# First attention of a chain of layers: first two head groups scored in fp32 on 32-row tiles, reads by group, causal mask by GpSimd selects, value products woven into the scores

## The chip, the cores and the metric

The program runs on one core of one Trainium2 chip. The time is the device time of one execution in microseconds; the median of several runs is compared. Engines are called PE (TensorE; PEld is its weight load), DVE (VectorE), ACT (ScalarE), POOL (GpSimd) and SP (SyncE, which issues most DMAs).

## What is computed

The reference is a chain of eight residual layers on one tensor x of 4 x 512 tokens and 128 channels. Only the first layer is touched by the change, a causal softmax attention with 16 heads of 8 channels (block-wise in the reference, which gives the same result):

```python
xn = layernorm(x)
q, k, v = (heads(xn @ W.T) for W in (Wq, Wk, Wv))      # 4 x 16 x 512 x 8
s = 8 ** -0.5 * q @ k^T, masked where the key is later than the query
x = x + (exp(s - max s) @ v / sum) @ Wo.T
```

Everything is fp32. The layers behind it (two mixtures of experts, a feature attention, a gated recurrence, a retention and two quantized feed-forward layers) stay as they are.

## The kernel before, in words

Each engine has a program of its own, written out by hand; the order of the calls in `attn_a_tensor`, `attn_a_vector`, `attn_a_scalar`, `attn_a_gpsimd` and `attn_a_sync` is the order of the work, and semaphores tie them. b is the batch block (4 of 512 tokens), a group n is four heads of one block (n // 4 the block, n % 4 the four heads), so there are 16 groups.

**Start.** For each b: layer norm on DVE (`norm_front` statistics, `norm_root` on POOL, `norm_back` with L117), transposes on PE (L127), copy by ACT (L135), projections of q and k (L168, `factors`) with channels as rows, copied by ACT (L448). The scores use bf16 with three terms: q and k are split into three bf16 parts (block 0 by DVE, L347 to L353, in line with its norms; blocks 1 to 3 by POOL, L518 to L524), written to a DRAM scratch (L558, L560) and read back (L546, L551), so that all 72 products of parts and channels of one head lie in 72 rows of `a_QS` and `a_KS`. Block 0 is read by group, blocks 1 to 3 whole: 1152 KB for q and three times 384 KB for k.

**One group.** `maxima` (L194, then L197) computes scores with queries as rows into PSUM bank 6 or 7 in turn, eleven jobs for a group, and adds the causal mask by a matmul of the identity with `neg_ts`; DVE reduces each job (L359) to its maximum, and its job frees the bank. `maxima_split` (L368 to L374) splits the maxima in three bf16 parts, `rows` transposes them (L208), `row_copy` (L381) copies them, and SP's `rows` brings them by three small DMAs (L583) into rows 72 to 74 of `a_QS`. Then `exps` and `tail` (L214) compute the scores with keys as rows, less the maximum, in banks 0 to 3 and 4, `late` (L218) adds the mask with `neg_st`, and ACT takes the exponential (L465, L470) into `a_PT`, six buffers. `values` (L252) multiplies with v and a column of ones, sixteen products on four 32-column tiles in one lump, into bank 5; ACT evicts (L478), `turned` transposes (L264), DVE normalizes (L388 to L392).

**The loop.** PE first computes the maxima of groups 0 and 1. Iteration n then scores group n, with the jobs of maxima n + 2, `rows(n + 1)`, `values(n - 1)` and `turned(n - 1)` between. DVE's list has the same order. Once for each block there are also the projection of v (`plain`), `back` (L273) and `output` (L282), the residual (L143) and the next layer's norm. SP's list in `attn_a_sync` is: rows(n + 1), then the write of block n + 2 (n = 0, 1), then the read of block 2 or 3 (n = 3, 7, after the last scores of the block two before). At its start SP loads x in four DMAs and then `pack_zero`, 2653.5 KB of constants for later layers, first read at `expert_bias` at the end of iteration 14.

Of the kernel before, what the change touches and what calls it, by code (L numbers as in the profile page):

```python
# [21 lines left out]
          "r_km": "a_f", "r_v": "a_exped", "r_ot": "a_ol", "r_raw": "a_ot", "f_rowt": "a_rowt"}  # L22
# [131 lines left out]

def side(M):

    M.sides[0] += 1
    return 6 + M.sides[0] % 2


def attn_a_tensor(pe, S, M):
    def factors(b):
        for name, w, bk in (("q", M.a_wq, 2 + 2 * (b % 2)), ("k", M.a_wk, 3 + 2 * (b % 2))):
            made = S["a_proj"]
            take(pe, M, bk)
# [46 lines left out]
    def scores(b, h, si, out, first=True):  # L212
        i = b % 2
        pe.matmul(out, M.a_KS[0:75, i, h, 128 * si:128 * si + 128], M.a_QS[0:75, i, h, 128 * si:512], start=first, stop=False, skip_group_check=True)  # L214

    def late(out):

        return pe.matmul(out, M.identb[:, :], M.neg_st[:, :].unsqueeze(1).to_broadcast([128, out.shape[1], 128]), start=False, stop=True,  # L218
                         skip_group_check=True)

    def exps(n, hh):
# [2531 lines left out]
```

## Time and profile before

| | |
|---|---|
| median of 3 runs | 1253.16 us (1251.23 to 1256.07) |
| profiled execution, its own time | 1249.02 us |
| its span | 1247.2 us |
| mean granted PE clock | 0.867 |
| busy PE / DVE / ACT / POOL | 1007.8 / 835.9 / 387.6 / 294.5 us |
| first attention in it | 0 to about 268.4 us |
| PE's granted clock by fortieths of the span, first ten | 8 6 8 9 9 8 9 9 8 9 tenths |

The granted clock is a share of 2.4 GHz; 0.50 is 1.2 GHz. A stretch with a value between has parts at either level. A busy engine is not an engine at its peak: PE's busy time counts overlapping matmuls once.

### The profile page before, as it was taken

To read this page: it belongs to the slowest core of one execution; us is meant where nothing else is said; L and a number is where in the kernel's file an instruction comes from. 1 tells how busy PE (TensorE), PEld (TensorE's weight loads), DVE (VectorE), ACT (ScalarE), POOL (GpSimd) and SP (SyncE) were. 2 spreads that over 40 slices of the span, in tenths; PEclk is the share of its full clock that TensorE was granted. 3 is DMA by queue.
4 is the path that set the end of the run, shared out by engine and by line. 5 is a ranking of instruction groups with operands and counts; after the bars stand their busy time and mean duration, and the time that the engine had idled before them with its cause. 6 is when DMAs were issued, how large, how long until landed. Compare 5 with 4: busy or idle time off the path is not lost.

```text
span 1247.2 us, 16823 instructions
## 1 busy us (share of the span) xinstructions
PE 1007.8 (81%) x6275; PEld 619.5 (50%) x6275; DVE 835.9 (67%) x2001; ACT 387.6 (31%) x634; POOL 294.5 (24%) x249
## 2 busy tenths in 40 slices
PE   3798988979989897679897862999999566897465
PEld 2254555543434565543333331776768345676344
DVE  5666758756565467767666566648555896688895
ACT  1154445533333243423232254112211222231121
POOL 3600000003222433303222213121110344233232
PEclk8689889989999787779888896899999887787786
DMA  8633030020000000000000000000000000000000
GB/s 239 161 103 78 2 78 2 3 89 1 1 1 0 1 2 1 2 1 0 1 1 0 1 0 3 1 1 1 1 1 2 0 1 1 2 2 2 1 9 25
DMA packets 9948, 25.40 MB, mean 20 GB/s; under 512 B 979, under 2 KB 7315, under 8 KB 9171
## 3 DMA queue, kind: packets, MB, share of 16 engines
q1 hardware_dynamic: 9568, 23.49, 6.6%
q10 hardware_dynamic: 294, 0.79, 0.3%
q8 instruction: 52, 0.85, 0.3%
q14 instruction: 34, 0.28, 0.1%
HBM read 16.73 MB, written 7.34 MB: 19 GB/s over the span
## 4 chain that ended last, share of the span: by engine, by line
PE 54%; DVE 31%; issue 6%; ACT 4%; POOL 3%; DMA 2%; DVEq 0%; SPq 0%; ACTq 0%; POOLq 0%
PE ps L686 5%; DVE a_MN L359 4%; PE ps L673 4%; PE ps L678 4%; PE ps L252 3%; PE ps L194 2%; DVE XN L117 2%; PE ps L1507 2%; PE ps L1568 2%; PE ps L1522 2%; PE ps L1565 2%; PE ps L2098 2%; PE ps L214 2%; PE ps L1940 2%; POOL rs L96 1%
## 5 line engine op out<-in xcount | busy, mean ns | idle before, releaser
L359 DVE TENSOR_REDUCE a_MN<-ps 128x1 f32<-128x384 f32 (+3 forms) x176 | 107.4, 639 | 59.6 <-PE ps L197 57.5
L96 POOL TENSOR_TENSOR rs<-t,mhalf 128x4 f32<-128x4 f32 x37 | 37.4, 1011 | 382.8 <-DVE t L90 382.5
L930 POOL TENSOR_TENSOR f_Y<-f_Y,f_TT 128x512 f32<-128x512 f32 x56 | 70.8, 1265 | 179.4 <-DVE f_TT L820 179.4
L465 ACT ACTIVATE a_PT<-ps 128x1024 f32<-128x1024 f32 x64 | 65.1, 1024 | 69.9 <-PE ps L218 68.9
L895 ACT ACTIVATE f_HH<-ps,pack_zero 128x512 f32<-128x512 f32 x64 | 44.0, 687 | 132.9 <-PE ps L673 132.9
L143 DVE TENSOR_TENSOR X<-ps,X 128x512 f32<-128x512 f32 x32 | 22.0, 687 | 92.7 <-PE ps L1578 49.4
L194 PE MATMUL ps<-a_KS,a_QS 72*128 72x128 bf16 (+3 forms) x256 | 70.5, 337 | 14.1 <-DVE a_MN L359 10.9
L686 PE MATMUL ps<-f_HH,pack_zero 128*128 128x512 f32 x128 | 73.9, 660 | 5.7 <-DVE f_TT L820 5.7
L811 DVE TENSOR_TENSOR f_XS<-ps,XNT 128x512 f32<-128x512 f32 x64 | 43.9, 688 | 49.2 <-PE ps L666 49.2
L673 PE MATMUL ps<-f_XS,pack_zero 128*128 128x512 f32 x128 | 69.9, 630 | 1.3 <-DVE f_XS L811 1.3
L820 DVE SCALAR_TENSOR_TENSOR f_TT<-ps,pack_zero,f_X 128x512 f32<-128x512 f32 x64 | 47.9, 749 | 32.5 <-PE ps L686 32.5
L1921 PE MATMUL ps<-pack_one,XNT 128*128 128x352 f32 x128 | 50.0, 539 | 23.4 <-DVE q_HH L1970 23.2
L678 PE MATMUL ps<-f_XS,pack_zero 128*128 128x512 f32 x128 | 68.5, 618 | 0.0
L214 PE MATMUL ps<-a_QS,a_KS 75*128 75x128 bf16 (+3 forms) x256 | 58.2, 316 | 6.1 <-DMA a_QS<-a_MT 5.9
L1940 PE MATMUL ps<-pack_one,q_HT 128*128 128x128 f32 (+1 forms) x192 | 36.1, 334 | 20.9 <-ACT q_HT L2023 20.9
L899 ACT ACTIVATE f_X<-ps 128x512 f32<-128x512 f32 x64 | 38.2, 597 | 33.0 <-PE ps L679 32.9
L1921 PEld LDWEIGHTS ps<-pack_one,XNT 128*128 128x128 f32 x128 | 27.1, 225 | 41.3 <-DVE q_HH L1970 27.6
L197 PE MATMUL ps<-pack_half 128*128 128x128 bf16 (+2 forms) x176 | 47.3, 269 | 0.0
L194 PEld LDWEIGHTS ps<-a_KS,a_QS 72*128 72x128 bf16 x256 | 23.2, 105 | 43.6 <-DVE a_MN L359 27.7
L1940 PEld LDWEIGHTS ps<-pack_one,q_HT 128*128 128x128 f32 (+1 forms) x192 | 29.3, 228 | 30.4 <-ACT q_HT L2023 23.4
L127 PE MATMUL ps<-pack_first,XN 128*128 128x128 f32 x80 | 16.5, 343 | 33.8 <-DVE XN L117 33.8
L252 PE MATMUL ps<-a_PT,a_VA 128*32 128x128 f32 (+3 forms) x512 | 42.2, 464 | 1.3 <-ACT a_PT L470 1.3
(310 smaller groups left out, 2322.4 us busy)
## 6 DMA issues: line engine op xcount, KB each, us to landing
scratch<-a_parts SPq DMA_DIRECT2D x16, 384.0 KB, 4.3
a_QS<-scratch SPq DMA_DIRECT2D x3, 1152.0 KB
a_KS<-scratch SPq DMA_DIRECT2D x9, 384.0 KB
pack_one<-in_one SPq DMA_DIRECT2D x1, 2679.5 KB, 9.3
pack_zero<-in_zero SPq DMA_DIRECT2D x1, 2653.5 KB, 16.3
a_QS<-scratch SPq DMA_DIRECT2D x4, 288.0 KB
a_KS<-scratch SPq DMA_DIRECT2D x12, 96.0 KB
X<-in_x SPq DMA_DIRECT2D x4, 256.0 KB, 10.1
```

What stands on the lines that cost most here:

```text
L96: pool.tensor_tensor(M.rs[:, 4 * b:4 * b + 4], M.t1[:, 4 * b:4 * b + 4], M.mhalf[:, 0:4], ALU.pow).then_inc(root.sem, root.tick(n, b))
L194: pe.matmul(bank(M, bk, N, N * u), M.a_QS[0:72, i, h, 128 * ti:128 * ti + 128], M.a_KS[0:72, i, h, 0:N], start=(u == 0), stop=False, skip_ ...
L214: pe.matmul(out, M.a_KS[0:75, i, h, 128 * si:128 * si + 128], M.a_QS[0:75, i, h, 128 * si:512], start=first, stop=False, skip_group_check= ...
L252: m = pe.matmul(bank(M, 5, N, 128 * si, 32 * j, 32 * j + 32), M.a_VA[:, i, si, 4 * g + j, :], M.a_PT[:, (4 * n + j) % 6, A_AT[si]:A_AT[si] ...
L359: dve.tensor_reduce(M.a_MN[:, n % 2, ti, h0:h0 + k], bank(M, M.bank["a_max", n, jj], 128 * (ti + 1) * k).rearrange("p (a c) -> p a c", a=k ...
L465: act.activation(M.a_PT[:, c % 6, 0:1024], M.ps[:, a * 512:a * 512 + 1024], ACT.Exp).then_inc(made.sem, made.tick(n, hh))
L673: pe.matmul(bank(M, 2 + u % 2), M.f_w1[:, e, :], M.f_XS[:, x, :], start=True, stop=True).then_inc(made.sem, made.tick(n, u, 1))
L678: pe.matmul(bank(M, 4), M.f_w3[:, e, :], M.f_XS[:, x, :], start=True, stop=False)
L686: pe.matmul(bank(M, 5), M.f_w2[:, e, :], M.f_HH[:, u % 3, :], start=True, stop=True).then_inc(made.sem, made.tick(n, u))
L930: pool.tensor_tensor(M.f_Y[:, i, :], M.f_Y[:, i, :], M.f_TT[:, u % 3, :], ALU.add).then_inc(made.sem, made.tick(n, u))
L1921: pe.matmul(bank(M, 2 * k + s, 352), M.XNT[:, 128 * t:128 * t + 128], M.WG[:, s, :], start=True, stop=True).then_inc(made.sem, made.tick(n ...
L1940: m = pe.matmul(bank(M, bo, 128, 128 * (t % 4)), M.q_HT[0:rows, t % 2, a, :], M.WD[0:rows, a, :], start=(a == 0), stop=(a == 2))
```

## The change

Five things change together in the first attention:

1. Groups 0 and 1 (block 0, heads 0 to 7) are computed without the bf16 parts and without DRAM. `own` projects q and k so that head j of the group lies in rows 32j to 32j + 7 of a tile; ACT copies them with a scale that zeroes the other rows and, for k, a bias that makes row 32j + 8 a row of ones. `own_maxima` multiplies in fp32 on 32-row tiles of PE (group 0 four heads at a time in banks 4 to 7, group 1 two in banks 6 and 7). DVE writes the maxima into column 32j + 8 of `a_MX`, fp32 transposes turn them (`own_rows`), and `own_add` adds them as row 32j + 8 of q. `own_exps` and `own_tail` score in fp32 on the same tiles.
2. Block 0's groups 2 and 3 and all later blocks still go through DRAM, but POOL now splits block 0 too, and every read is of one group (`a_spread`); for groups 8 to 15 it stands behind rows(n + 1) of iteration n = group - 5. `pack_zero` is loaded in three parts behind the rows DMAs of groups 12 to 14.
3. The mask matmuls on the scores (`late`) are gone; POOL zeroes the masked part of the exponentials instead (`seen`: per group four selects of 128 x 256 and two of 128 x 512 elements).
4. `a_PT` has eight buffers for six; `values(n - 1)` is divided into its four key blocks, one behind each head's scores; `turned`, `evict` and `normalize` come one iteration later, and `back`, `output`, `residual`, the transposes of the next layer likewise one group later.
5. At the start DVE computes the statistics of all blocks first; the norm, transposes and projections of blocks 2 and 3 are placed between the groups.

The core of the diff ("..." where left out):

```diff
+    def own(g, name, bk):
+        made, w = S["a_proj"], M.a_oq if name == "q" else M.a_ok
+        M.bank["a_own", g, name] = bk
+        take(pe, M, bk)
+        pe.matmul(bank(M, bk), w[:, 8 * g:8 * g + 128], M.XNT[:, 0:512], start=True, stop=True).then_inc(made.sem, made.tick("own", g, name))
+        M.freed[bk] = (S["a_own"], (g, name))
...
+    def own_maxima(n, part, heads, banks):
+        maxed = S["a_maxed"]
+        for j, bk in zip(heads, banks):
+            M.bank["a_max", n, part, j] = bk
+            take(pe, M, bk)
+        pe.wait_ge(S["a_own"].sem, S["a_own"].at(n, "k"))
+        at = 0
+        for ti in A_FIRST[part]:
+            N = 128 * (ti + 1)
+            for j, bk in zip(heads, banks):
+                row = slice(32 * j, 32 * j + 8)
+                pe.matmul(bank(M, bk, N, at), M.a_Q4[row, n, 128 * ti:128 * ti + 128], M.a_K4[row, n, 0:N],
+                          start=(at == 0), stop=False, skip_group_check=True)
+            at += N
+        for j, bk in zip(heads, banks):
+            tiles = bank(M, bk).rearrange("p (a c) -> p a c", a=4)
+            ends = (tiles[:, 3:4, :], tiles[:, 0:4:3, :], tiles[:, 1:2, :])[part]
+            k = len(A_FIRST[part])
+            pe.matmul(ends, M.identb[:, :], M.neg_ts[:, :].unsqueeze(1).to_broadcast([128, k, 128]), start=False, stop=True,
+                      skip_group_check=True).then_inc(maxed.sem, maxed.tick(n, part, "own", j))
+            M.freed[bk] = (S["a_reduced"], (n, part, "own", j))
...
+    def own_scores(n, j, si, out):
+        row = slice(32 * j, 32 * j + 9)
+        return pe.matmul(out, M.a_K4[row, n, 128 * si:128 * si + 128], M.a_Q4[row, n, 128 * si:512], start=True, stop=True)
...
+    def own_exps(n, half):
+        scored = S["a_scored"]
+        for bk in range(4):
+            take(pe, M, bk)
+        pe.wait_ge(S["a_mt"].sem, S["a_mt"].at(n))
+        for u in range(2):
+            own_scores(n, 2 * half + u, 0, bank(M, 2 * u))
+        for u in range(2):
+            own_scores(n, 2 * half + u, 1, bank(M, 2 * u + 1, 384))
+        for u in range(2):
+            hh = 2 * half + u
+            own_scores(n, hh, 3, bank(M, 2 * u + 1, 128, 384)).then_inc(scored.sem, scored.tick(n, hh))
+            M.freed[2 * u] = M.freed[2 * u + 1] = (S["a_exped"], (n, hh))
...
+        if jj == 0:
+            pe.wait_ge(S[f"a_spread{n % 4}{i}"].sem, S[f"a_spread{n % 4}{i}"].at(b))
...
         scores(b, h, 0, bank(M, a))
-        late(bank(M, a, 128).unsqueeze(1))
         scores(b, h, 1, bank(M, a + 1, 384))
-        scores(b, h, 3, bank(M, a + 1, 128, 384), False)
-        late(bank(M, a + 1).rearrange("p (a c) -> p a c", a=4)[:, 0:4:3, :]).then_inc(scored.sem, scored.tick(n, hh))
...
+    def values(n, si):
+        b, g, i, valued, N = n // 4, n % 4, n // 4 % 2, S["a_valued"], 512 - 128 * si
+        if si == 0:
+            take(pe, M, 5)
+            if g == 0:
+                pe.wait_ge(S["a_va"].sem, S["a_va"].at(b))
+            pe.wait_ge(S["a_seen"].sem, S["a_seen"].at(n, "tail", 1))
+        for j in range(4):
+            m = pe.matmul(bank(M, 5, N, 128 * si, 32 * j, 32 * j + 32), M.a_VA[:, i, si, 4 * g + j, :],
+                          M.a_PT[:, (4 * n + j) % 8, A_AT[si]:A_AT[si] + N],
+                          start=(si == 0), stop=(si == 3), skip_group_check=True)
+        if si == 3:
+            m.then_inc(valued.sem, valued.tick(n))
+            M.freed[5] = (S["a_ol"], (n,))
...
+    own_maxima(0, 0, range(4), range(4, 8))
+    factor(0, "q", 3)
+    factor(0, "k", 0)
+    own_maxima(0, 1, range(4), range(4, 8))
+    own(1, "q", 1)
+    own(1, "k", 2)
+    own_maxima(0, 2, range(4), range(4, 8))
+    plain(0, 3)
+    turn_tensor(pe, S, M, 0, 1, 0, M.XN, (S["normed"], (0, 1)))
+    factor(1, "q", 1)
+    factor(1, "k", 2)
+    own_rows(0, 5)
+    own_exps(0, 0)
+    own_maxima(1, 0, (0, 1), (6, 7))
+    own_tail(0, 0, 0)
+    own_maxima(1, 0, (2, 3), (6, 7))
+    own_tail(0, 0, 1)
+    own_maxima(1, 1, (0, 1), (6, 7))
+    own_exps(0, 1)
+    own_maxima(1, 1, (2, 3), (6, 7))
+    own_tail(0, 1, 0)
+    own_maxima(1, 2, (0, 1), (6, 7))
+    own_tail(0, 1, 1)
+    own_maxima(1, 2, (2, 3), (6, 7))
+    own_rows(1, 5)
+    turn_tensor(pe, S, M, 0, 2, 0, M.XN, (S["normed"], (0, 2)))
+    factor(2, "q", 2)
+    factor(2, "k", 3)
     pe.wait_ge(S["in_ones"].sem, 16)
     for jj in range(11):
-        maxima(0, jj)
-    for jj in range(6):
-        maxima(1, jj)
-    rows(0)
+        maxima(2, jj)
+    own_exps(1, 0)
+    maxima(3, 0)
+    own_tail(1, 0, 0)
+    values(0, 0)
+    own_tail(1, 0, 1)
+    maxima(3, 1)
+    values(0, 1)
+    plain(1, side(M))
+    for jj in range(2, 6):
+        maxima(3, jj)
+    rows(2)
+    own_exps(1, 1)
+    values(0, 2)
+    own_tail(1, 1, 0)
+    values(0, 3)
+    own_tail(1, 1, 1)
     for jj in range(6, 11):
-        maxima(1, jj)
...
+        maxima(3, jj)
+    turn_tensor(pe, S, M, 0, 3, 0, M.XN, (S["normed"], (0, 3)))
+    factor(3, "q", 2)
+    factor(3, "k", 3)
+    for n in range(2, 16):
+        b, g, ahead = n // 4, n % 4, range(11) if n + 2 < 16 else range(0)
+        for hh in range(4):
+            for jj in ahead[3 * hh:3 * hh + 1]:
+                maxima(n + 2, jj)
+            exps(n, hh)
+            for jj in ahead[3 * hh + 1:3 * hh + 2]:
+                maxima(n + 2, jj)
+            if hh % 2:
+                tail(n, hh // 2)
+            if hh == 1 and n + 1 < 16:
+                rows(n + 1)
+            values(n - 1, hh)
+            for jj in ahead[3 * hh + 2:3 * hh + 3]:
+                maxima(n + 2, jj)
+            if hh == 0 and g == 1 and b + 1 < 4:
+                plain(b + 1, side(M))
+            if hh == 0 and g == 2 and b:
+                back(b - 1)
+            if hh == 1:
+                turned(n - 2)
+            if hh == 2 and g == 2 and b:
+                output(b - 1)
+            if hh == 3 and g == 3 and b:
+                turn_tensor(pe, S, M, 1, b - 1, side(M), M.XN, (S["normed"], (1, b - 1)))
+    turned(14)
+    for si in range(4):
+        values(15, si)
...
+    norm_back(dve, S, M, 0, 1, M.X, M.XN)
+    norm_back(dve, S, M, 0, 2, M.X, M.XN)
+    for part in range(3):
+        for j in range(4):
+            own_reduce(0, part, j)
+    own_add(0)
+    for part in range(3):
+        for j in range(4):
+            own_reduce(1, part, j)
+    own_add(1)
+    norm_back(dve, S, M, 0, 3, M.X, M.XN)
     for jj in range(11):
-        reduce(0, jj)
-    maxima_split(0)
+        reduce(2, jj)
+    maxima_split(2)
     for jj in range(6):
-        reduce(1, jj)
-    row_copy(0)
+        reduce(3, jj)
+    row_copy(2)
     for jj in range(6, 11):
-        reduce(1, jj)
-    maxima_split(1)
-    for n in range(16):
+        reduce(3, jj)
+    maxima_split(3)
+    for n in range(2, 16):
         b, g, more = n // 4, n % 4, n + 2 < 16
         if more:
-            for jj in range(6):
+            for jj in range(5):
                 reduce(n + 2, jj)
         if n + 1 < 16:
             row_copy(n + 1)
+        if more:
+            reduce(n + 2, 5)
+        if g == 3 and b:
+            norm_back(dve, S, M, 1, b - 1, M.X, M.XN)
+        normalize(n - 2)
...
+    def own(g):
+        made, proj = S["a_own"], S["a_proj"]
+        act.wait_ge(proj.sem, proj.at("own", g, "q"))
+        act.activation(M.a_Q4[:, g, :], bank(M, M.bank["a_own", g, "q"]), ACT.Identity, scale=M.a_o3[:, 0:1]).then_inc(made.sem, made.tick(g, "q"))
+        act.wait_ge(proj.sem, proj.at("own", g, "k"))
+        act.activation(M.a_K4[:, g, :], bank(M, M.bank["a_own", g, "k"]), ACT.Identity, bias=M.a_o3[:, 2:3],
+                       scale=M.a_o3[:, 1:2]).then_inc(made.sem, made.tick(g, "k"))
...
+    def seen(n, half):
+        made, c = S["a_seen"], 4 * n + 2 * half
+        for u in range(2):
+            P = M.a_PT[:, (c + u) % 8, 0:1024].rearrange("p (a t) -> p a t", a=2)[:, :, 0:128]
+            pool.wait_ge(S["a_exped"].sem, S["a_exped"].at(n, 2 * half + u))
+            pool.affine_select(P, P, [[0, 2], [1, 128]], ALU.is_ge, 0.0, base=0, channel_multiplier=-1).then_inc(made.sem, made.tick(n, 2 * half + u))
+        P = M.a_PT[:, c % 8:c % 8 + 2, 896:1152].rearrange("p h (a t) -> p h a t", a=2)
+        pool.wait_ge(S["a_exped"].sem, S["a_exped"].at(n, "tail", half))
+        pool.affine_select(P, P, [[0, 2], [0, 2], [1, 128]], ALU.is_ge, 0.0, base=0, channel_multiplier=-1).then_inc(made.sem, made.tick(n, "tail", half))
...
+    for b in range(2):
         split(b, "q")
         split(b, "k")
-    for b in range(4):
-        norm_root(pool, S, M, 1, b)
+    for n in range(2):
+        for half in range(2):
...
+    written(0)
+    read(2)
+    read(3)
     write(1)
-    read(1)
-    rows(0)
-    for n in range(15):
+    written(1)
+    for n in range(4, 8):
+        read(n)
+    for n in range(1, 15):
         rows(n + 1)
-        if n in (0, 1):
-            write(n + 2)
-        if n in (3, 7):
-            read(n // 4 + 2)
+        if n in (1, 2):
+            write(n + 1)
+        if n == 3:
+            written(2)
+        if n == 7:
+            written(3)
+        if 3 <= n < 11:
+            read(n + 5)
+        if n >= 11 and n < 14:
+            zeros(n - 11)
...
```

## Rows read from the trace of the kernel before

**Rows 1.** Busy time by stretches: us; PE, PEld, DVE, ACT, POOL; clock, DMA share, GB/s.

```profile
11.25:41.00 29.75, 16.70 (x38) 7.80 (x39) 17.17 (x59) 6.46 (x11) 13.62 (x16) 0.73 0.81 261
...
41.00:59.10 18.10, 14.70 (x64) 4.96 (x62) 15.38 (x28) 0.60 (x1) 10.59 (x12) 0.59 0.62 132
...
59.10:83.40 24.30, 22.94 (x160) 13.96 (x159) 15.87 (x35) 11.55 (x14) 0.00 (x0) 0.79 0.35 114
...
239.50:268.40 28.90, 24.70 (x213) 18.06 (x214) 14.74 (x67) 12.63 (x18) 2.01 (x2) 0.86 0.13 46
```

**Rows 2.** Timeline of the start: start us, us, operation, [idle before <-releaser].

```profile
22.94 1.11 PE L127 MATMUL ps<-pack_first,XN 128*128 128x128 f32 x4 [7.10 <-DVE XN L117]
...
37.26 3.75 PE L168 MATMUL ps<-XNT,pack_first 128*128 128x512 f32 x4 [0.78 <-ACT XNT L135]
...
39.96 0.15 PEld L194 LDWEIGHTS ps<-a_KS,a_QS 72*128 72x128 bf16 x1 [0.52 <-issue]
```

**Rows 3.** Timeline: first scores of iterations 2, 3, 14; values and reduce in 2.

```profile
83.34 0.38 PE L214 MATMUL ps<-a_QS,a_KS 75*128 75x512 bf16 x1
...
87.67 2.32 PE L252 MATMUL ps<-a_PT,a_VA 128*32 128x512 f32 x29
...
90.35 0.56 DVE L359 TENSOR_REDUCE a_MN<-ps 128x1 f32<-128x384 f32 x1 [2.00 <-PE ps L197]
...
94.57 0.38 PE L214 MATMUL ps<-a_QS,a_KS 75*128 75x512 bf16 x1
...
240.55 0.38 PE L214 MATMUL ps<-a_QS,a_KS 75*128 75x512 bf16 x1
```

**Rows 4.** Groups by line, 83 to 239.7 us: | busy, mean ns | idle before.

```profile
L359 DVE TENSOR_REDUCE a_MN<-ps 128x1 f32<-128x512 f32 (+3 forms) x133 | 81.3, 639 | 43.6 <-PE ps L197 42.1
...
L218 PE MATMUL ps<-pack_half 128*128 128x256 bf16 (+1 forms) x120 | 31.5, 262 | 0.0
...
L381 DVE COPY a_MT<-ps 12x512 bf16<-12x512 bf16 x12 | 4.9, 412 | 0.5 <-PE ps L208 0.4
...
L392 DVE TENSOR_TENSOR a_ON<-ps,a_RS 128x128 f32<-128x128 f32 x12 | 3.5, 291 | 0.4
...
L390 DVE RECIPROCAL a_RS<-a_RS 128x16 f32<-128x16 f32 x12 | 3.0, 253 | 0.4
...
L117 DVE TENSOR_SCALAR XN<-X,mv,rs 128x128 f32<-128x128 f32 x8 | 2.2, 343 | 0.1
...
L370 DVE TENSOR_TENSOR a_MR<-a_MN,a_M 128x16 f32<-128x16 f32 x12 | 2.1, 175 | 0.4
```

**Rows 5.** The chain that ended last: start us, us, what.

```profile
112.09 8.85 DMA a_QS<-a_MT
...
168.81 9.17 DMA a_QS<-a_MT
```

**Rows 6.** Timeline of SP's queue.

```profile
104.83 0.33 SPq L546 DMA_DIRECT2D a_QS<-scratch  x1
```

**Rows 7.** Busy time by stretches of 2 us, at the first stall.

```profile
118.00:120.00 2.00, 0.27 (x2) 0.00 (x0) 1.49 (x6) 0.00 (x0) 0.00 (x0) 1.00 0.41 88
```

**Rows 8.** Timeline, PE's weight loads, another stage.

```profile
428.86 1.78 PEld L978 LDWEIGHTS ps<-pack_zero,p_QT 32*128 32x128 f32 x16 [1.50 <-issue]
...
430.87 1.78 PEld L989 LDWEIGHTS ps<-pack_zero,XNT 128*128 128x128 f32 x8 [0.23 <-issue]
```

**Rows 9.** Groups by line and shape, POOL, whole span.

```profile
L1261 POOL TENSOR_SCALAR p_PK<-p_XW 128x512 f32<-128x512 f32 x16 | 23.8, 1490 | 45.5 <-ACT p_XW L1180 45.0
...
L2362 POOL COPY r_VA<-pack_zero 128x128 f32<-128x128 f32 x16 | 4.9, 348 | 6.2 <-ACT pack_zero L2319 6.2
```

**Rows 10.** Timeline, DVE beside POOL's split.

```profile
31.59 3.66 DVE L117 TENSOR_SCALAR XN<-X,mv,rs 128x128 f32<-128x128 f32 x4
...
41.91 4.07 DVE L359 TENSOR_REDUCE a_MN<-ps 128x4 f32<-128x512 f32 x7 [6.66 <-PE ps L197]
...
49.46 1.01 DVE L372 CAST a_M<-a_MR 128x16 bf16<-128x16 f32 x1
```

More of the change, by code:

```diff
@@ L180, in maxima, with own_tail @@
+    def own_tail(n, half, u):
+        scored, landed = S["a_scored"], S["a_landed"]
+        if u == 0:
+            take(pe, M, 4)
+            own_scores(n, 2 * half, 2, bank(M, 4, 256)).then_inc(landed.sem, landed.tick(n, half))
+        else:
+            pe.wait_ge(landed.sem, landed.n)
+            own_scores(n, 2 * half + 1, 2, bank(M, 4, 256, 256)).then_inc(scored.sem, scored.tick(n, "tail", half))
+            M.freed[4] = (S["a_exped"], (n, "tail", half))
     def maxima(n, jj):
@@ L210, in rows, with scores @@
         M.freed[bk] = (S["a_mt"], (n,))
-    def scores(b, h, si, out, first=True):
+    def scores(b, h, si, out):
         i = b % 2
[L214 to L219, printed above, removed]
+        return pe.matmul(out, M.a_KS[0:75, i, h, 128 * si:128 * si + 128], M.a_QS[0:75, i, h, 128 * si:512], start=True, stop=True)
     def exps(n, hh):
@@ L497, in attn_a_scalar @@
             tail(n, half)
-            if half == 0:
-                if n:
-                    evict(n - 1)
-                if g == 0 and b + 1 < 4:
-                    plain(b + 1)
-                if g == 1 and b:
-                    back(b - 1)
-                if g == 3 and b:
-                    turn_scalar(act, S, M, 1, b - 1)
+            if n == 1 and half == 0:
+                plain(1)
+        turn_scalar(act, S, M, 0, n + 2)
+        factors(n + 2)
+    for n in range(2, 16):
+        b, g = n // 4, n % 4
+        evict(n - 2)
+        exps(n, 0)
+        if g == 1 and b + 1 < 4:
+            plain(b + 1)
+        if g == 2 and b:
+            back(b - 1)
+        exps(n, 1)
+        tail(n, 0)
+        exps(n, 2)
+        exps(n, 3)
+        tail(n, 1)
+        if g == 3 and b:
+            turn_scalar(act, S, M, 1, b - 1)
+    evict(14)
     evict(15)
@@ L533, in attn_a_gpsimd @@
         norm_root(pool, S, M, 0, b)
-    for b in range(1, 4):
+    for b in range(2):
         split(b, "q")
         split(b, "k")
-    for b in range(4):
-        norm_root(pool, S, M, 1, b)
+    for n in range(2):
+        for half in range(2):
+            seen(n, half)
+        split(n + 2, "q")
+        split(n + 2, "k")
+    for n in range(2, 16):
+        b, g = n // 4, n % 4
+        for half in range(2):
+            seen(n, half)
+        if g == 2 and b:
+            norm_root(pool, S, M, 1, b - 1)
+    norm_root(pool, S, M, 1, 3)
 def spread_rows(sp, b, name, scr, dst, done, event, heads=slice(0, 16)):
```

243 lines of the change are left out of this document (104 added, 139 removed).

## The prediction, made before the change was run

> **What bounds the kernel now.** I read the busy time by stretches first, because the change touches only the first attention, 0 to 268.4 us of the 1247.2 us span. The reader should see four stretches in [rows 1]: the start to the first maxima (11.25 to 41.0), the maxima of groups 0 and 1 ahead of the loop (to 59.1), iterations 0 and 1 (to 83.4), and the tail (239.5 to 268.4, 28.9 us). TensorE (PE) was granted 0.73, 0.59 and 0.79 in the first three: much of the start ran at 1.2 GHz.
>
> Then the timeline of the start [rows 2]. PE sat idle 7.10 us before block 1's transposes, because VectorE (DVE) splits q and k of block 0 before it normalizes block 1. But the first maxima's weights load at 39.96, straight behind the last projections (37.26 plus 3.75), with no wait for a DMA. So the bounce through DRAM is not what the start waits for; the order of work on PE and DVE is.
>
> Then one iteration [rows 3]. The first scores of iterations 2 and 3 start 11.23 us apart, those of iteration 14 at 240.55. So iterations 2 to 13 took 157.2 us: 12 x 11.23 = 134.8, and 22.4 more. In each iteration the values matmuls are one lump of 2.3 us, and DVE idles 2.00 us behind it. The groups by line [rows 4] give DVE's own work in one iteration: eleven reduces 6.7 us (81.3 x 11 / 133), row copy 0.41, normalize 0.25 + 0.29 and a small one as the split's (0.175), split 4 x 0.175: 8.5, and 8.9 with the gaps of 0.03 to 0.05 between dependent ones.
>
> Last the stalls: the chain holds two row DMAs of 8.85 and 9.17 us [rows 5]. SP issued the read of block 2 at 104.83 [rows 6], 2.3 MB, and DMA was still at 0.41 busy in 118 to 120 [rows 7]; the 12 KB of rows(5) queued behind it. No scores of iteration 5 could start before they landed.
>
> **The change, part by part.**
> *Start.* The DVE split goes to POOL, which nobody needs before group 2. The first own projections start at 11.25 as the others do now and take 3.75, as in [rows 2]; with ScalarE's (ACT) copy of 0.6 they are there at 15.6. A maxima job of four 32-row tiles is a cost the trace lacks. The nearest rows [rows 8]: 16 weight loads of 32-row fp32 pairs took 1.78 us, 8 loads of full fp32 tiles the same 1.78 us, so a pair costs what one full matmul costs. I take tiles of different rows as parallel: 1.0 us for 512 columns at 2.4 GHz and 2.0 at 1.2, for a pair or for four; the other end is one after the other, 0.49 us more for each further tile and pass pair. Part 0 is thus done at about 18; DVE by then has normalized blocks 1 and 2. Three parts go back and forth between PE (2.3, 1.9, 1.3 at mixed clock) and DVE (6.7 in all), with projections between: the reduces end at 29. Values projection 1, transposes 1.1, copy 0.6, projections of block 1 3.2, row transposes 1 and the add 0.7: the scores of group 0 start at 36.5, where they started at 59.1.
> *Groups 0 and 1.* What was gained is then spent. Scoring one group costs 6.2 us of PE in fp32 (per half 2.1 for the pairs plus 1.0 for two single tails) where bf16 took some 3. Group 1's maxima come in pairs, and each pair must be reduced (two heads, 1.4 us, plus 0.25 of latency) before the next enters banks 6 and 7: with the scores between them 17 to 18 us for this section. Then, each in PE's line: transposes and projections of block 2 (3.4), the maxima of group 2 (8), the scores of group 1 woven with values 0 and the maxima of group 3 (16), and block 3 (3.2). Sum: 36.5 + 17.7 + 3.4 + 8 + 16 + 3.2 = 85, and 2 for stretches at 1.2 GHz: iteration 2 starts at 87, 4 later than now. Bounds: 77 if little of the alternation shows, 95 if it is all at 1.2 GHz.
> *Steady loop.* Ten mask matmuls go: 31.5 us over 12 iterations by busy time, some 0.85 us of streaming in each. They are PE's, and DVE has the longer list, so alone they would give little. The weave gives more: the 2.3 us lump becomes pieces of 0.9, 0.65, 0.45 and 0.2. Walking one iteration, PE may do about 0.4 us of other work between two maxima jobs without starving DVE (a reduce of 0.6 to 0.69 less a job of 0.2 to 0.3). Over it are the first piece (hidden under the split), the second with rows and tail (0.25 us of DVE idle), and turned (0.1). So 8.9 + 0.5 to 0.7: 9.5. Two costs come on top. Values of n-1 wait for POOL's last select: exp ends, 0.1 later the select, then PE. An affine select is in no row; the nearest one-input POOL rows are a copy of 128 elements at 348 ns and a TENSOR_SCALAR of 512 at 1490 ns [rows 9]. By these ends 256 elements cost 0.35 to 0.75 us or, by an operation slower than both, more. I take 0.5 for 256 and 0.9 for 512, nearer to the copy since nothing is computed but a choice: the values start some 0.5 late, 0.4 of it felt. And POOL, now 4 x 0.5 + 2 x 0.9 = 3.8 us busy in each iteration, can hold DVE (next part): 0.2. That makes 10.1.
> *Extras in iterations 2 to 13.* Residual, norm front and back for two blocks (some 4 each, of which the four normalize instructions 1.4 [rows 4]), plain projections and the wait of normalize 0 for POOL's split of block 3: 12. Total 12 x 10.1 + 12 = 133 against 157.2.
> *Reads.* They move to quarters (576 KB, at 14.5 us per 2.3 MB about 3.6 us) behind rows(n+1) in SP's queue; each is done about when the next rows are issued, 10 us later. SP's wait before group 8's read (end of iteration 3) is over before row copy 5. I cost them at nothing, covered by some 1 us of slack; at the other end 0.5 us in each of 8 iterations. The 2.65 MB of constants move behind rows 12 to 14, in three parts of some 5 us; needed at the end of iteration 14: nothing.
> *Tail.* Iterations 14 and 15 have no maxima and stay as now: from 240.55 [rows 3] to 268.4, the end of the last stretch in [rows 1], 27.9. The last select stands before values 15: +0.5, so 28.4.
>
> Sum: start 87 + 133 + 28.4 = 248.4 against 268.4: **20 us less**. The profiled execution took 1249.0 (span 1247.2); the median of three is 1253.2. It stands 4 above, so I forecast 1253.2 - 20 = **1233** and give all times on the median's scale.
>
> **The rule weighed.** In [rows 10] DVE's four normalize instructions took 3.66 us and one 16-element cast 1.01 us while POOL split q and k; the same take 4 x 0.343 and 0.175 elsewhere [rows 4]. Seven reduces out of PSUM beside the same POOL work took 4.07, 0.58 each, no more than their mean of 0.64. My sum has 0.2 us an iteration for it, since POOL is busy for 3.8 of 10; without it the sum gives 1231, and with every second split instruction held 1251 (a rival below). The Trainium skill (SBUF — State Buffer, section "Who interferes with whom") says that a DVE copy, cast or tensor_scalar and a GpSimd instruction lock each other out for a whole instruction, and tensor_reduce never; by that rule, the trace agrees, and the selects are a cost to DVE and not only to POOL.
>
> **Rivals.**
> *The start gains too* and the loop sits at DVE's floor: iteration 2 at 79, iterations of 9.3: 8 + 9.6 less than my sum, **1215**. For: PE is fed earlier. Against: the pairs' alternation.
> *PE and DVE stay in step*: the pieces of values land where a bank is awaited, and iterations keep 10.9. The two stalls still go: 12 x 10.9 + 12 = 143: **1243**. For: DVE idles in six places of an iteration now, only one of them the lump.
> *Select against split*: POOL's selects hold the four split instructions and the normalize as in [rows 10], 0.84 us each for one in two: 1.7 us an iteration, 1.5 more than in my sum, 12 times: **1251**, no change. For: the four stand at the end of DVE's list, when the exponentials of a group end. Against: POOL was busy all the time in those rows. This is the rule of the Trainium skill's page SBUF — State Buffer biting in full.
> *Row tiles don't overlap*: 512-column pairs take 1.7 and fours 3.5; some 16 us more for groups 0 and 1: **1249**. For: that both kinds in [rows 8] may be bound by weight loads.
> *Slower*: POOL paces the loop. All select work is 8 times a 256-element select. Above 1.47 us for one (11.8 per iteration) the gain is gone; at 2 us the iterations take 16: 12 x 5.9 more, **1304**. For: POOL's costs vary widely between operations. Against: none with one input is above 3 ns per element.
> *That the change doesn't do what it says*: the bounce's removal gives nothing at the start, as shown. That is in my sum.
>
> **How the numbers follow.** Forecast 0.42, start gains too 0.24, in step 0.13, select against split 0.08, row tiles 0.05, POOL paces 0.08. The range takes the start's bounds (-10, +8) and the loop's (9.3 to 10.9 an iteration): 1205 to 1252, leaving out the last case and the far end of the second. A measurement tells 0.5% (6.3 us) from no change. Faster: the first three cases nearly whole, 0.79; same 0.12; slower 0.09.
>
> **What would show it.** Group 0's scores at 36 to 37; iteration 2 at 83 to 91; iterations of about 10 us without a DMA of 9 us in the chain; the DVE idle behind values gone; selects of 0.5 and 0.9. I am wrong if a 256-element select exceeds 1.4 us, if 32-row pairs space at 0.43 us per weight load and more, if iteration 2 comes before 78 or after 96, or if row DMAs still hold PE.

## The result, and the profile after

The median after is **1262.28 us** (1253.98 to 1265.96, 19 runs) against 1252.41 (1241.88 to 1262.71, 19 runs) of the kernel before on the same chip: ratio **1.0067** [1.0044, 1.0091]. The change is slower by 0.7%, about 10 us, where 20 us of gain were forecast. The profiled execution took 1262.28 (span 1260.4, clock 0.848) against 1249.02 (1247.2, 0.867).

Busy time by stretches after: start, first section of groups 0 and 1, the rest ahead of iteration 2, iterations 2 to 13, tail (columns as in [rows 1]).

```profile
11.25:34.59 23.34, 17.80 (x77) 8.08 (x77) 14.38 (x60) 6.51 (x11) 11.44 (x13) 0.85 0.35 106
34.59:57.40 22.81, 20.88 (x77) 9.25 (x77) 6.92 (x16) 5.07 (x6) 8.59 (x13) 0.58 0.71 188
57.40:103.30 45.90, 42.67 (x150) 17.86 (x151) 17.83 (x40) 8.65 (x12) 10.31 (x15) 0.54 0.10 35
103.30:244.30 141.00, 129.73 (x1045) 60.23 (x1043) 111.06 (x260) 70.34 (x91) 42.42 (x80) 0.94 0.23 64
244.30:278.40 34.10, 27.19 (x205) 16.54 (x202) 16.76 (x70) 14.22 (x21) 8.94 (x16) 0.83 0.14 49
```

Read against [rows 1] and [rows 3]. Iteration 2 starts at 103.3 in place of 83.3: **20.0 later** (103.3 is its first maxima job; its first scores are at 103.75, 20.4 later). Iterations 2 to 13 take 141 in place of 157.2: **16 less**. The tail takes 34.1 in place of 27.9: **6 more**. Sum 10. The spans differ by 13.2; the other 3 lie behind the stage. What follows it took 978 to 987 us in the profiled executions of all kernels here; no edit touches it. In the second and third stretch the clock is 0.58 and 0.54 although PE is busy for 63.6 of 68.7 us.

The first maxima of group 0, then the section behind them, in PE's timeline (start us, us, operation):

```profile
15.74 1.14 PE L203 MATMUL ps<-a_QS 8*128 8x512 f32 x8 [0.96 <-ACT a_QS L575]
...
34.59 1.99 PE L226 MATMUL ps<-a_QS 9*128 9x512 f32 x12 [0.88 <-DVE a_QS L458]
36.39 1.05 PE L203 MATMUL ps<-a_QS 8*128 8x512 f32 x4
...
39.03 2.08 PE L203 MATMUL ps<-a_QS 8*128 8x512 f32 x4 [0.73 <-DVE a_OL L450]
...
45.30 3.79 PE L226 MATMUL ps<-a_QS 9*128 9x512 f32 x12
48.88 1.92 PE L203 MATMUL ps<-a_QS 8*128 8x128 f32 x8
...
57.40 0.88 PE L221 MATMUL ps<-pack_first,a_OL 128*128 128x128 f32 x3 [0.83 <-DVE a_OL L450]
```

Group 0's scores start at 34.59, the forecast was 36.5. The same six products (twelve records, two heads on two tiles) take 1.99 us there and 3.79 eleven us later; a 512-column pair of the maxima takes 1.05 and then 2.08. The chain that ended last shows the rest (start us, us, what):

```profile
60.12 3.75 PE ps L171 x4
...
71.10 3.71 PE ps L226 x12
...
87.42 3.72 PE ps L226 x12
...
109.36 1.16 POOL a_parts L664
...
116.00 1.07 PE ps L314 x8
...
126.08 1.07 PE ps L314 x8
```

Projections and group 1's scores all run at the lower level; the loop then turns in 10.08 us (116.00 to 126.08; 11.23 before), and no row DMA stands in the chain from 100 to 250 us. POOL's split of block 3 does (102.94 to 110.5): it holds `normalize(0)`, and iteration 2 takes 11.2 us. The groups by line from 105 to 244 us:

```profile
L464 DVE TENSOR_REDUCE a_MN<-ps 128x1 f32<-128x384 f32 (+3 forms) x131 | 80.7, 638 | 23.4 <-PE ps L267 21.9
...
L477 DVE CAST a_M<-a_MR 128x16 bf16<-128x16 f32 x11 | 4.9, 443 | 0.4
...
L475 DVE TENSOR_TENSOR a_MR<-a_MN,a_M 128x16 f32<-128x16 f32 x11 | 2.8, 258 | 0.4
...
L473 DVE CAST a_M<-a_MN 128x16 bf16<-128x16 f32 x11 | 2.3, 206 | 1.1
...
L673 POOL TENSOR_SCALAR_AFFINE_SELECT a_PT<-a_PT 128x256 f32<-128x256 f32 x47 | 19.1, 406 | 91.1 <-ACT a_PT L593 91.1
...
L676 POOL TENSOR_SCALAR_AFFINE_SELECT a_PT<-a_PT 128x512 f32<-128x512 f32 x23 | 14.8, 643 | 1.9
```

The reduces cost what they did in [rows 4], with the idle time ahead of them halved (43.6 to 23.4). The selects took 0.41 and 0.64 us. Three of DVE's four split instructions now take 443, 258 and 206 ns where each took 175 before: 0.38 us more in each iteration. The tail, PE's timeline:

```profile
254.55 1.07 PE L314 MATMUL ps<-a_PT,a_VA 128*32 128x512 f32 x8 [1.33 <-POOL a_PT L676]
...
260.70 0.63 PE L127 MATMUL ps<-pack_first,XN 128*128 128x128 f32 x4 [0.84 <-DVE XN L117]
262.60 0.63 PE L327 MATMUL ps<-pack_first,a_OL 128*128 128x128 f32 x4 [1.27 <-ACT a_OL L606]
263.16 4.05 PE L314 MATMUL ps<-a_PT,a_VA 128*32 128x512 f32 x32
...
271.15 2.05 PE L345 MATMUL ps<-pack_first,a_f 128*128 128x128 f32 x8 [0.84 <-ACT a_f L613]
```

### The profile page after: what moved, and what is told of

The parts are those of the page before. It is cut to its first block, busy times and chain, and to the rows that moved or that the text cites. A ratio compares the mean times of both kernels' runs of the same rounds, so it can differ in the third digit from the quotient of the medians.

```text
span 1260.4 us, 16766 instructions
## 1 busy us (share of the span) xinstructions
PE 1038.1 (82%) x6189; PEld 613.3 (49%) x6189; DVE 832.8 (66%) x1995; ACT 388.4 (31%) x638; POOL 349.2 (28%) x354
## 4 chain that ended last, share of the span: by engine, by line
PE 59%; DVE 29%; issue 5%; ACT 3%; POOL 3%; DMA 1%; DVEq 0%; ACTq 0%; SPq 0%; POOLq 0%
PE ps L862 5%; PE ps L849 4%; PE ps L854 3%; PE ps L314 3%; PE ps L264 3%; DVE a_MN L464 2%; DVE q_E L1483 2%; PE ps L2274 2%; PE ps L1744 2%; PE ps L1683 2%; DVE XN L117 2%; PE ps L1698 2%; PE ps L1741 2%; PE ps L1154 2%; PE ps L226 1%
## 5 line engine op out<-in xcount | busy, mean ns | idle before, releaser
L464 DVE TENSOR_REDUCE a_MN<-ps 128x1 f32<-128x384 f32 (+3 forms) x154 | 95.1, 639 | 50.4 <-PE ps L267 48.6
L264 PE MATMUL ps<-a_KS,a_QS 72*128 72x128 bf16 (+3 forms) x224 | 61.1, 333 | 12.7 <-DVE a_MN L464 5.6
L849 PE MATMUL ps<-f_XS,pack_zero 128*128 128x512 f32 x128 | 68.5, 618 | 1.3 <-DVE f_XS L987 1.3
L854 PE MATMUL ps<-f_XS,pack_zero 128*128 128x512 f32 x128 | 66.5, 601 | 0.0
L673 POOL TENSOR_SCALAR_AFFINE_SELECT a_PT<-a_PT 128x256 f32<-128x256 f32 x64 | 25.9, 406 | 125.7 <-ACT a_PT L593 125.6
L314 PE MATMUL ps<-a_PT,a_VA 128*32 128x128 f32 (+3 forms) x512 | 53.7, 492 | 2.3 <-POOL a_PT L676 2.1
L264 PEld LDWEIGHTS ps<-a_KS,a_QS 72*128 72x128 bf16 x224 | 19.5, 103 | 63.7 <-DVE a_MN L464 41.3
L284 PE MATMUL ps<-a_QS,a_KS 75*128 75x512 bf16 (+1 forms) x224 | 45.7, 310 | 0.0
L2116 PEld LDWEIGHTS ps<-pack_one,q_HT 128*128 128x128 f32 (+1 forms) x192 | 29.3, 228 | 30.5 <-ACT q_HT L2199 23.5
L1941 POOL TENSOR_TENSOR h_RN<-h_N,mhalf 128x32 f32<-128x32 f32 x4 | 21.7, 5431 | 77.6 <-DVE h_N L1800 77.6
```

Of the source, the lines that this page charges most:

```text
L264: pe.matmul(bank(M, bk, N, N * u), M.a_QS[0:72, i, h, 128 * ti:128 * ti + 128], M.a_KS[0:72, i, h, 0:N], start=(u == 0), stop=False, skip_ ...
L284: return pe.matmul(out, M.a_KS[0:75, i, h, 128 * si:128 * si + 128], M.a_QS[0:75, i, h, 128 * si:512], start=True, stop=True)
L314: m = pe.matmul(bank(M, 5, N, 128 * si, 32 * j, 32 * j + 32), M.a_VA[:, i, si, 4 * g + j, :], M.a_PT[:, (4 * n + j) % 8, A_AT[si]:A_AT[si] ...
L464: dve.tensor_reduce(M.a_MN[:, n % 2, ti, h0:h0 + k], bank(M, M.bank["a_max", n, jj], 128 * (ti + 1) * k).rearrange("p (a c) -> p a c", a=k ...
L849: pe.matmul(bank(M, 2 + u % 2), M.f_w1[:, e, :], M.f_XS[:, x, :], start=True, stop=True).then_inc(made.sem, made.tick(n, u, 1))
L854: pe.matmul(bank(M, 4), M.f_w3[:, e, :], M.f_XS[:, x, :], start=True, stop=False)
```

## The experiments

"Iteration 2 at" below is the start of its first exponentials in ACT's timeline (104.5 after, 84.2 before), "stage end" the end of the last norm (278.4 after, 268.4 before). A and B are the two theories of each expectation. Where two of these kernels are compared, their medians come from different chips, on which the kernel before took 1252.4 to 1256.3 us; the ratios, each to the kernel before on the same chip, allow for that.

**First set: the start.** Two small edits of the changed kernel, then its loop behind the old start.

```diff
-                row = slice(32 * j, 32 * j + 8)
+                row = slice(32 * j, 32 * j + 32)
```

> The changed kernel with the products of the first two groups over all 32 rows of their tiles (the added rows hold zeros) in place of 8 or 9. Theory A: the start is slow because PE stands at 1.2 GHz from 39 to 103 us, and it does so because the fp32 products use only 8 or 9 rows of each tile. Then 32 rows bring the granted clock of 40 to 100 us from about 0.52 to near 1.0, iteration 2 starts 10 to 20 us earlier, and the time falls by as much, to about 1245. Rival B: what PE does in those tiles does not depend on the rows in use (the clock follows something else, or the alternation with DVE costs the time): clock and time as in the changed kernel, 1262 within 3.

(`own_scores` likewise.) 1256.33 (ratio 1.0020 [0.9996, 1.0044]); iteration 2 at 101.9, the clock in 40 to 100 us still 0.50 to 0.67. More rows of the same tiles do not lift the clock. The median is 6 below that of the change, but only 2.6 of it lie in the stage (end 275.8).

```diff
-        if n == 14:
+        if n == 15:
             expert_bias(dve, S, M)
```

(in iteration 15 it stands behind `normalize(13)`.)

> The changed kernel with the thirteen small DVE instructions of the expert bias moved from the end of iteration 14 to iteration 15, behind the norm of block 2 and normalize 13. Theory A: the tail is 6 us longer than before because the bias (253.7 to 258.5 us) stands in front of the norm that PE's last transposes wait for, values 15 wait behind these, and they then run at 1.2 GHz. Then the stretch from the first scores of iteration 14 to the last norm falls from 34.0 to 28 to 30 us and the time by 4 to 6, to 1257. Rival B: the tail is longer because of the selects before values 15 and the turned that comes one iteration later: under 1.5 us less.

1256.26 (1.0018 [0.9996, 1.0040]), stage end 276.6: 1.8 earlier, of which 0.5 lie ahead of iteration 2. Values 15 still took 3.96 us. Here too most of the median's 6 us lie behind the stage. The expert bias in front of the norm is a small part of the longer tail.

```diff
-    own(0, "q", 1)
...
-    for n in range(2, 16):
+    for b in range(4):
+        turn_tensor(...)
...
+    for n in range(16):
```

(shown in part; start of before, with DVE's split of block 0 and all groups through DRAM, by group; the loop of after.)

> The start of the kernel before (DVE splits block 0, all groups through DRAM, maxima of groups 0 and 1 ahead) with the loop of the changed kernel (selects, values woven, eight buffers, reads by group, late constants), now over iterations 0 to 15. Theory A: the fp32 groups cost 20 us at the start and the loop gains 16: the first scores of iteration 2 come at 81 to 84 us, clean iterations stay 10.1, no row DMA stalls, the time is 1240 to 1243, below both kernels. Rival B: the loop's gain hangs on what the fp32 groups leave out (POOL's split and DMA traffic of block 0, two groups less to read and write): the stalls or slower iterations return and the time is 1250 or more.

**1239.77** (1239.06 to 1242.79), ratio **0.9899** [0.9859, 0.9939]. Iteration 2 at 84.3, stage end 255.8. The start alone costs the change 20.2 us; with it taken back the rest gains 1%. The same times as above:

```profile
34.59:57.40 22.81, 17.73 (x65) 6.39 (x66) 14.89 (x27) 1.79 (x3) 16.46 (x19) 0.60 0.73 194
57.40:83.00 25.60, 25.03 (x136) 11.83 (x135) 17.13 (x34) 10.13 (x12) 4.76 (x10) 0.62 0.24 78
```

The clock is low here too (0.60, 0.62). So a low clock is not special to the fp32 start. What differs is how much PE work lies in it: 63.6 us busy from 34.59 to iteration 2, here 42.8.

> The kernel with the start of before and the changed loop, and the expert bias one iteration later as well. Theory A: both terms add: 4 to 6 us below the one without the move, 1236 to 1238. Rival B: the bias was hidden in that kernel: no difference between the two.

(this start and the later bias together.) 1238.29 (0.9887 [0.9846, 0.9928]), iteration 2 at 83.0, stage end 254.2. Only 1.5 less than with the bias in iteration 14, which is inside the interval.

**Second set: the clock, and the parts of the loop.**

```diff
     own_maxima(1, 0, (0, 1), (6, 7))
+    full()
+    full()
```

(eleven such pairs in the first section; each `full` is a bf16 product of the 128-row identity with 512 columns of the mask, into bank 5, which nobody reads.)

> The changed kernel with two more bf16 products over the whole array (128 rows, 512 columns, into the free bank 5) behind each of the eleven steps between the first scores of group 0 and the row transposes of group 1: 22 in all, 4.7 us of streaming at 2.4 GHz or 9.4 at 1.2. Theory A: small products do not keep PE's clock up, however long its busy time, and work over the whole array does. Then the granted clock from 40 to 57 us is near 1.0 and that section takes no longer than its 22.8 us in spite of the added work, or less. Rival B: the clock follows the idle gaps between steps or something else: it stays at 0.50 and the section takes 25 to 32 us.

1265.88 (1.0101 [1.0068, 1.0134]), iteration 2 at 112.2. The 22 products added PE time (11.5 us busy), and the clock stayed low: 0.50 in 40 to 60 us.

```diff
-                row = slice(32 * j, 32 * j + 8)
+                row = slice(0, 128)
```

(the same for `own_scores`; each product then sums over the four heads of its group.)

> The changed kernel with the products of the first two groups over all 128 rows, so that each sums over the four heads (the output of these heads is another one), and tiles no longer run side by side. Theory A (whole-array work raises the clock): granted clock near 1.0 in most of 40 to 100 us; the columns double for pairs and quadruple for fours but at twice the clock, so that iteration 2 starts within 5 us of 103. Rival B: the clock stays at 0.50 in 40 to 100 and the start takes 15 to 30 us longer.

1256.42 (1.0008 [0.9978, 1.0038]), iteration 2 at 96.0: 8.5 earlier than after, though the four heads can no longer share the array. From group 1's row transposes to the first scores of iteration 2 it is 34.4 us in place of 46.3 (57.40 to 103.75):

```profile
60.80 0.63 PE L221 MATMUL ps<-pack_first,a_OL 128*128 128x128 f32 x4 [0.88 <-DVE a_OL L450]
...
95.22 0.60 PE L284 MATMUL ps<-a_QS,a_KS 75*128 75x512 bf16 x3
```

What is gained there does not last: iterations 2 and 3 take 13.8 and 10.8 us for 11.2 and 10.1 after (the clock was 0.50 in 105 to 110), the lead is 3.8 at iteration 14, and the stage ends at 275.3, 3.1 earlier than after and 0.5 earlier than with 32 rows. The stretches of this kernel, then of the one with 22 full products:

```profile
34.00:57.00 23.00, 19.34 (x72) 10.65 (x73) 6.11 (x13) 5.68 (x7) 9.32 (x13) 1.00 0.73 186
57.00:95.00 38.00, 32.15 (x169) 15.98 (x168) 18.94 (x44) 9.27 (x13) 10.70 (x16) 0.96 0.21 59
```

```profile
34.00:63.00 29.00, 28.61 (x89) 10.65 (x90) 6.41 (x15) 4.56 (x6) 8.35 (x12) 0.56 0.63 165
```

With row tiles PE was busy for 28.61 of 29.00 us at 0.56; with products over all rows for 19.34 of 23.00 us at 1.00. A busier PE had the lower clock. Group 0's first maxima, four products of 512 columns, took 1.14 us on four tiles (above); over 128 rows, at 2.4 GHz as well:

```profile
16.17 3.67 PE L203 MATMUL ps<-a_QS 128*128 128x512 f32 x8 [0.96 <-ACT a_QS L575]
```

```diff
-            if n:
-                values(n - 1, hh)
+            if n and hh == 1:
+                for si in range(4):
+                    values(n - 1, si)
```

> The kernel with the start of before, the changed loop and the later bias (1238.3 us, clean iterations of 10.1), but the value products of a group in one lump behind the rows, as in the kernel before. Theory A: the weave is what shortens an iteration, from 11.2 to 10.1, since DVE idled 2 us behind the lump: iterations go back to 10.8 to 11.0 and the time rises by 9 to 13, to 1248 to 1251. Rival B: the masks that left PE shorten it: iterations stay at 10.1 to 10.3, the time within 3 of 1238.

1263.41 (1.0056 [1.0025, 1.0086]), 25 above the woven form (21 by the ratios; the stage ends at 273.4, 19 later) and well above A's 1248 to 1251. The lump in its chain, first at the low clock, then at the high one:

```profile
90.44 4.28 PE ps L314 x30
...
103.65 2.21 PE ps L314 x30
```

```diff
+    def late(out):
+        return pe.matmul(out, M.identb[:, :], M.neg_st[:, :]..., start=False, stop=True)
...
-        for half in range(2):
-            seen(n, half)
```

> The same kernel (start of before, changed loop, later bias), but the causal mask of the scores by ten matmuls a group on PE and no selects. Theory A: the masks are 0.85 us of PE's streaming in each iteration where DVE has the longer list, and the selects cost DVE up to 0.6 us by holding its small instructions: iterations change by -0.2 to +0.4, the time is 1236 to 1243. Rival B: PE is the longer list once the values are woven: iterations of 10.9, time 1248.

1243.21 (0.9904 [0.9866, 0.9941]), 5 above selects (2 by the ratios, whose intervals overlap; the stage ends at 261.3, 7 later), at the upper edge of A's range.

**Third set: the second group, the reads, the lump again.**

```diff
     own_exps(0, 0)
-    own_maxima(1, 0, (0, 1), (6, 7))
+    for jj in range(3):
+        maxima(1, jj)
...
-    for n in range(2, 16):
+    for n in range(1, 16):
```

> Group 0 alone in fp32 on 32-row tiles; group 1 goes through DRAM like all later ones, its bf16 maxima stand between the scores of group 0, and the loop begins with iteration 1. Expert bias in iteration 15 as in the second run. To be held against start by DRAM with the bias later (1238.3, first exponentials of group 0 at 59.0, of iteration 1 at 70.8, of iteration 2 at 83.0). Theory A, the fp32 start loses by the second group, whose maxima go in pairs through two banks at a clock of 0.50, while the parts of block 0 are back from DRAM by about 35: group 0's first exponentials at 34 to 37, iteration 1's at 63 to 67, the time 4 to 7 us below, 1231 to 1235. Theory B, any fp32 group on row tiles leaves the clock at 0.50 for what follows until the loop runs: iteration 1's first exponentials at 71 to 76, the time 1238 to 1243.

1237.07 (1234.53 to 1247.08, 4 runs; 0.9879 [0.9797, 0.9961]). Group 0's last exponentials start at 52.0, iteration 2 at 83.2, as in the kernel by DRAM (83.0). With the bias as here and both groups in fp32 it was 104.0: the second fp32 group alone is the loss of 20. But the first one gains nothing either, as B had it: its lead of 21 us over the bounce (37.6 against 59.0) is gone by iteration 2.

```diff
-        if 3 <= n < 11:
-            read(n + 5)
+        if n in (3, 7):
+            for m in range(n + 5, n + 9):
+                read(m)
```

> Start by DRAM, bias later (1238.3), but blocks 2 and 3 are read whole in iterations 3 and 7 as in the kernel before. Theory A, the two row DMAs of 8.85 and 9.17 us in the chain of before were waits behind that read: both come back in the chain with 7 to 9 us each and hold the scores of iterations 5 and 9, the time goes up by 10 to 16 us, 1248 to 1254. Theory B, the row DMAs are late for another reason or the woven loop has slack for them: up by less than 4, below 1242.

1248.12 (0.9958 [0.9921, 0.9995]), 9.8 above the kernel with reads by group (8.9 by the ratios); stage end 267.0 against 254.2, of which 2.3 were there at the first exponentials. The wait is back in its chain:

```profile
112.55 8.49 DMA a_QS<-a_MT
...
169.28 5.44 DMA a_QS<-a_MT
```

The medians' difference is just under A's 10 to 16; the mechanism is A's.

> Start by DRAM, bias later, masks as matmuls on PE, values in one lump: the loop of before with reads by group and turned, evict and normalize one iteration later. Held against masks on PE with woven values (1243.2) and lump with selects (1263.4). Theory A, the lump costs what it did in before (2 us of DVE idle behind it in each iteration of 11.2), and the 18 us that it cost with selects were the lump waiting for POOL's last select: 12 to 14 iterations of 1.0 us more than woven, 1253 to 1258. Theory B, the lump costs the same 18 to 25 us with either mask: 1261 to 1268.

(the edits of the lump and of the masks on PE together.) 1258.18 (1.003 [0.999, 1.007]), A's upper end. The stage ends at 271.1, 10 later than with masks on PE and woven values; 4 more lie behind it in the traces. Undisturbed iterations, by ACT's timeline of first exponentials, with all groups read singly:

| | masks on PE | selects on POOL |
|---|---|---|
| values in a lump | 11.3 | 11.1 |
| values woven | 10.5 | 10.1 |

The weave gives 0.8 to 1.0 us an iteration, the selects 0.2 to 0.4. With selects the lump cost more than that: 7.4 us of it in iterations 1 and 2 (15.3 and 14.4 us for 12.2 and 10.1), where the lump ran at the low clock (4.28 us above), and 15 in iterations 3 to 13.

**Last: the clock behind the lead of group 0.** The edit of the 128-row products on the kernel with group 0 alone.

> As group 0 alone in fp32 (1237.1; iteration 2's first exponentials at 83.2; clock 0.50 in 40 to 50 us and 0.56 in 50 to 60), with its own products over all 128 rows: each gives the sum over the four heads of the group, so the output is not the attention's. Theory A, the low clock behind the products on row tiles is what eats group 0's lead of 21 us: the clock is 1.00 in 40 to 60, projections of block 2 take 2.0 us in place of 3.7, group 0's first exponentials come at 41, iteration 2's at 76 to 79, the time 1230 to 1234. Theory B, four times the streaming of group 0 costs what the clock gives, or DVE's reduces of groups 1 and 2 set the pace at either clock: iteration 2's at 81 to 86, the time 1235 to 1241.

1232.09 (1229.94 to 1233.75, 4 runs; 0.9833 [0.9778, 0.9889]), in A's range, 5 below. But the two intervals overlap, and the traces show less: iteration 2 at 80.6, between the two theories and 2.6 earlier, stage end 252.8 for 255.1. The clock was 1.00 and 0.97 only from 40 to 60 us, and from 50 on DVE was busier than PE; behind that the clock fell here too:

```profile
50.00:60.00 10.00, 6.89 (x36) 3.15 (x36) 8.81 (x22) 2.77 (x5) 5.77 (x8) 0.97 0.78 197
60.00:70.00 10.00, 9.06 (x29) 3.54 (x28) 4.84 (x12) 1.79 (x3) 3.80 (x5) 0.52 0.04 9
```

PE's timeline with row tiles (1.2 GHz), then with 128 rows (2.4 GHz):

```profile
43.89 3.78 PE L226 MATMUL ps<-a_QS 9*128 9x512 f32 x12
...
54.81 3.75 PE L171 MATMUL ps<-XNT,pack_first 128*128 128x512 f32 x4 [0.78 <-ACT XNT L135]
```

```profile
44.96 3.67 PE L226 MATMUL ps<-a_QS 128*128 128x512 f32 x12
...
52.98 1.96 PE L171 MATMUL ps<-XNT,pack_first 128*128 128x512 f32 x4 [0.78 <-ACT XNT L135]
```

The six products of two heads take 3.78 us on two tiles; the same six one after another over the whole array take 3.67. What the tiles gain by running together is lost at the low clock, and the projections behind pay too (3.75 against 1.96).

## Why the prediction was wrong

**The step that failed is "Groups 0 and 1"**, in its clause "and 2 for stretches at 1.2 GHz". By its own terms, forecast and measured: scores of group 0 at 36.5, measured 34.6; first section 17.7, measured 22.8; transposes and projections of block 2 3.4, measured 6.6 with the row transposes (57.4 to 64.0); maxima of group 2 8, measured 7.1; group 1 woven with values 0 and maxima of group 3 16, measured 27.3 (71.1 to 98.4); block 3 3.2, measured 4.9; allowance 2. That is 103.3 for 87, outside the bound of 95 as well. I had counted most of it at 2.4 GHz; from 40 to 100 us PE had 0.50 to 0.67. The bound of 95 allowed 8 us more for the low clock; the woven stretch alone ran 11.3 over its term. The prices were right (1.05 and 2.08 us for a pair, forecast 1.0 and 2.0; four tiles in 1.14): the share of the work that would run at 1.2 GHz was not. [Rows 1] should have warned: the stretches of before stood at 0.59 and 0.79 in just these times, and the start by DRAM shows 0.60 to 0.62 with the new loop.

Two readings of the trace after put most of the 16.3 on the clock and not on the alternation of pairs. From 34.59 to 103.3 PE was idle for 5.2 us in all, so waits for DVE hold no more than that. And rows seen at both levels give an estimate of what the low one cost PE: three half groups of scores 3 x (3.79 - 1.99), seven tails 7 x (1.22 - 0.71), projections of blocks 2 and 3 1.8 and 1.5, values 0 2.2, values projection 1.0, together 15, the maxima not counted. What a higher clock would give back is another matter. With 128-row products, which cost at 2.4 GHz what pairs cost at 1.2, the stretch to iteration 2 was 11.9 shorter and iteration 2 came 8.5 earlier, but the stage ended only 3.1 earlier; with group 0 alone it was 2.6 and 2.4. No run has row tiles at 2.4 GHz throughout, so how the 20 us divide between the lower clock and the mere number of fp32 products stays open. That the second group is where it hurts rests on group 0 alone: 1237 for 1262, iteration 2 at 83.2 for 104.0.

**Loop: right in mechanism and in the iteration, too low in the extras.** Clean iterations were forecast at 10.1 and took 10.08. The stalls went, and came back when the whole reads did: worth 10 us. Extras were 12 in the sum and measured 141 - 12 x 10.08 = 20. By the first exponentials iterations 7 and 11 took 16.5 and 17.0: `norm_back` stands ahead of `normalize` on DVE, and PE waits for the bank of `turned` (1.68 us at 167.46 in the after trace). I had added instruction times and no wait behind them.

**Selects:** 0.41 and 0.64 us for 0.5 and 0.9. They are no pace-setter, and the rival of POOL is dead. In the loop they are worth 0.2 to 0.4 us an iteration.

**Rule against trace:** the rival had 1.7 us an iteration for splits and normalize held by selects, my sum 0.2. Measured: 0.38, from the splits of 443, 258 and 206 ns above; normalize took what it did before. The Trainium skill (SBUF — State Buffer, "Who interferes with whom") names the exclusion; the trace agrees that it is there, and here its price was small.

**Tail: 28.4 forecast, 34.1 measured.** I added one select and missed that `turned`, `evict` and `normalize` one iteration later put two groups' ends behind the last scores. Counted from iteration 14's first exponentials the tail took 27 before, 29.9 with lumps and masks on PE (so without selects, but with these calls one iteration later), 29.4 with lumps and selects, and 30.5 to 34 woven (33.2 after). Of the 33.2, 2.6 are clock: after, values 15 took 4.05 us and the output products 2.05; in the start by DRAM, with the same order of work, 2.36 and 1.13, and its tail took 30.5. What sets the level there was not tried.

Errors of the three terms: start 16.3, loop 8, tail 5.7, together 30; the median came out 29 above the forecast. None of my rivals was it: the slower one put the loss on POOL; the start did not gain (103.3); tiles do overlap (1.14, 1.99); and iterations of 10.08 rule out the two that kept them at 10.9 or more. My own sign of being wrong, iteration 2 after 96, came true. The range was also not what its terms give: 10 and 9.6 us below 1233 make 1213 and not 1205.

**The version that beats both:** the change without its fp32 start, 1238 to 1240 us, 1.0 to 1.1% below before. Group 0 in fp32 besides is no better within its interval.

## What to carry to other kernels

Count work that is moved into a stretch at the clock that the trace shows in that stretch, and take the lower level for all of it as the bound. When a change starts something 24 us earlier, follow it to the next point where both versions do the same work (here iteration 2) before booking a gain, and then to the end of the stage: a lead of 8.5 us at iteration 2 was 3.1 there. Of several edits in one change, time the steady part and the start separately: here they had opposite signs.

## What the runs showed of the hardware

- fp32 products on 32-row tiles do run together. Four of 512 columns on four tiles took 1.14 us at 2.4 GHz (15.74 us) where over 128 rows they took 3.67 (16.17 us), 3.2 times as long; six on two tiles took 1.99 (34.59 us) for 3.67 (44.96 us), 1.84 times. The Trainium skill (TensorE: Matmul & The Clock Gate, the part on packing small matmuls) gives 3.07 for four row tiles; the trace agrees. At 1.2 GHz the six took 3.78 us: nothing was left of the gain.
- PE's granted clock was 0.50 in several stretches in which it was busy nearly all the time with products on row tiles (9.83 of 10 us from 40 to 50), and 22 full bf16 products between them changed nothing; with every such product over 128 rows it was 1.00 at a lower busy share. Row tiles are not the only work at the low level: the start by DRAM had 0.60 and 0.62, and group 0 over 128 rows 0.52 from 60 to 70. Why, no run here tells.
- A GpSimd select of 128 x 256 fp32 elements took 0.41 us, of 128 x 512 0.64.
